# Layer 2 of a two-layer graph network: the projection of 400 turned nodes a product, with a copy and transposes behind it

## The chip, the cores and the metric

The kernel runs on one core of one Trainium2 chip. The metric is the device time of one execution in microseconds. The five engines are TensorE (PE in the profile; PEld are its weight loads), VectorE (DVE), ScalarE (ACT), GpSimd (POOL) and SyncE (SP), which only starts transfers here.

## What is computed

50,000 nodes with 128 features each and 50,000 edges, sorted by their target, go through two layers. Layer 1 is attention over the edges. Layer 2, which the change touches, is this (cut to what matters):

```python
def _L1_gnn_ref(node_features, senders, receivers, edge_features, W_kernel, W_bias, We_kernel, We_bias):
    hW = node_features @ W_kernel + W_bias
    h_self, h = jnp.split(hW, 2, axis=-1)
    send_edges = h[senders]
    send_edges = send_edges + (edge_features @ We_kernel + We_bias)
    in_degree = jax.ops.segment_sum(jnp.ones_like(receivers), receivers, num_nodes).astype(jnp.float32)
    send_edges = send_edges * jnp.clip(in_degree[receivers], 1, None)[..., None]
    return h_self + jax.ops.segment_sum(send_edges, receivers, num_nodes)

h = jnp.maximum(_layernorm(x, axis=-1), 0.0)
x = x + _L1_gnn_ref(h, src, dst, edge_attr_64, ...)
```

All in float32.

## The kernel before, in words

The nodes are cut into 500 tiles of 100 nodes, and ten tiles make a batch: 50 batches (`BATCHES`), numbered k. A tile's edges lie in one window of 128 edges. Three stages follow each other: a table of keys and values for all nodes, layer 1, and layer 2.

Since sums over edges and matrix products can change places, layer 2 first sums the raw rows that the edges bring and projects afterwards. A matrix `member` (128 edges x 100 nodes, the node's degree where edge and node belong together) does the sum. For a batch k of layer 2:

- SP loads the batch's own rows of x (`nodes1`) and the ten windows of edge features (`features`, L679, ten transfers, each with an address from a register loaded before it), two batches ahead. It stores the batch before it (`store1`, L690) when DVE's `sums` are through. It takes these in order: nodes1(k+2), registers and features(k+2), store1(k-1).
- POOL gathers the source rows of each tile (`gathers1`, L784), one indirect transfer a tile, into four slots. A pair of gathers waits until ACT has used the slot's old rows, so the gathers of k+4 go at the pace of ACT in k.
- ACT normalizes and clips a tile's own rows (L1576) and its gathered rows (L1579). It works one batch ahead of PE into single buffers `hn1` and `hs1`: the tiles 2j and 2j+1 of the next batch wait for `rows_sum(k, j)`, through the semaphore R.ha.
- PE makes in `rows_sum(k, j)` for two tiles the transposed own rows (L1869) and the summed gathered rows (L1870), in `features_sum(k, i)` for five tiles the summed edge features (L1858), and in `project1(k, g)` the result: for each tile three products into one place, with the turned rows as weights and W1 or We moving (L1884 to L1886). The groups g hold the tiles 0 to 3, 4 to 7, and 8 and 9 (`FOURS`).
- DVE makes `member` for the batch after (L1271), copies what rows_sum and features_sum left in PSUM to SBUF (`rows_out`, L1280; `features_out`, L1288), and adds x to the projected result (`sums`, L1298).

Every engine's order is written out by hand in its `step1`; nothing is planned at run time. PE's is: features_sum(k, 0), rows_sum(k, 0), project1(k-1, 2), rows_sum(k, 1), features_sum(k, 1), rows_sum(k, 2), project1(k, 0), rows_sum(k, 3), rows_sum(k, 4), project1(k, 1). DVE's is, with pairs of `member` between: features_out(k, 0), rows_out(k, 0), sums(k-1, 2), rows_out(k, 1), features_out(k, 1), rows_out(k, 2), rows_out(k, 3), sums(k, 0), rows_out(k, 4), sums(k, 1). Project1(k, g) waits for rows_out (R.ha_sb), features_out (R.ae_sb) and for the sums of two groups before (R.y).

On PE the batches 2 to 45 run in a loop of eleven turns over four batches; the others, and all batches on the other engines, are written out. In PSUM the eight banks are used so: rows_sum 0 and 1, features_sum 2 and 3, project1 4 and 5. Banks 6 and 7 are free in layer 2.

Of the kernel before, what the change touches and what calls it, by code (L numbers as in the profile page):

```python
# [16 lines left out]
NODES = 100  # L17
# [69 lines left out]


def rows_used(n):

    return 3 * (n // 5) + (1, 1, 2, 2, 3)[n % 5] if n >= 0 else 0


def features_used(n):

    return 3 * (n // 2) + (2, 3)[n % 2] if n >= 0 else 0
# [38 lines left out]
def build(nc, x, edges, ea, Wq, bq, Wk, bk, Wv, bv, Ws, bs, W1, b1, We, be, out):  # L135
# [7 lines left out]
    with ExitStack() as ctx:  # L143
# [89 lines left out]
        haT = hT_raw[:, 0:4 * 4 * NODES].rearrange("c (s t h n) -> c s t h n", s=4, t=2, h=2)  # L233
        aeT = mT_raw[0:EW + 1, 0:4 * 5 * NODES].rearrange("c (s t n) -> c s t n", s=4, t=5)
# [174 lines left out]
        class Message:  # L409


            def __init__(self):
# [10 lines left out]
                self.ae_sb = s("features_copied")  # L423
                self.out = s("out_ready")
# [369 lines left out]
        def _(dve):  # L794
# [481 lines left out]
            def rows_out(k, j):  # L1276
                n = 5 * k + j
                dve.wait_ge(R.ha, n + 1)
                wait(dve, R.out, rows_used(n - 4))
                dve.tensor_copy(haT[:, n % 4, :, :, :],  # L1280
                                banks[n % 2][:, 0:4 * NODES].rearrange("c (t h n) -> c t h n", t=2, h=2)
                                ).then_inc(R.ha_sb, 1)

            def features_out(k, i):
                n = 2 * k + i
                dve.wait_ge(R.ae, n + 1)
                wait(dve, R.out, features_used(n - 4))
                dve.tensor_copy(aeT[0:EW, n % 4, :, :],  # L1288
                                banks[2 + n % 2][0:EW, 0:5 * NODES].rearrange("c (t n) -> c t n", n=NODES)
                                ).then_inc(R.ae_sb, 1)  # L1290

            def sums(k, g):
                first, last = FOURS[g]
                dve.wait_ge(R.out, 3 * k + g + 1)
                if g == 0:
# [3 lines left out]
                                  banks[4 + (3 * k + g) % 2][0:NODES, 0:(last - first) * D]  # L1299
# [3 lines left out]
            def step1(k):  # L1303
                this, prev, nxt = real(k), real(k - 1), real(k + 1)
                if this:
                    features_out(k, 0)
                    rows_out(k, 0)
                if nxt:
                    members1(k + 1, 0, 2)
                if prev:  # L1310
                    sums(k - 1, 2)
                if this:
                    rows_out(k, 1)
                    features_out(k, 1)
                if nxt:
# [5 lines left out]
                if this:  # L1321
                    rows_out(k, 3)
                    sums(k, 0)
# [6 lines left out]
                if this:  # L1330
                    sums(k, 1)
# [301 lines left out]
        def _(pe):  # L1633
# [228 lines left out]
            def rows_sum(s, j):  # L1862
# [4 lines left out]
                for t in (2 * j, 2 * j + 1):  # L1867
                    at = (t % 2) * 2 * NODES
                    nc.tensor.transpose(banks[n % 2][:, at:at + NODES], hn1[:, t, :], ident[0:NODES, 0:NODES])  # L1869
                    ins = nc.tensor.matmul(banks[n % 2][:, at + NODES:at + 2 * NODES], hs1[:, t, :],  # L1870
# [3 lines left out]
            def project1(s, g):  # L1874
# [3 lines left out]
                pe.wait_ge(R.ae_sb, s.count(2, (1, 2, 2)[g]))  # L1878
                wait(pe, R.y, s.count(3, g - 1))
                ps = banks[4 + (3 * k + g) % 2]  # L1880
                for t in range(first, last):
                    to = ps[0:NODES, (t - first) * D:(t - first + 1) * D]
                    n = (5 * k + t // 2) % 4
                    nc.tensor.matmul(to, haT[:, n, t % 2, 0, :], w1[:, 0:D], start=True, stop=False)  # L1884
                    nc.tensor.matmul(to, haT[:, n, t % 2, 1, :], w1[:, D:2 * D], start=False, stop=False)  # L1885
                    ins = nc.tensor.matmul(to, aeT[:, (2 * k + t // 5) % 4, t % 5, :], weaug[0:EW + 1, 0:D],  # L1886
                                           start=False, stop=True)
                ins.then_inc(R.out, 1)

            def step1(s):  # L1890
# [5 lines left out]
                if prev:  # L1896
                    project1(before, 2)
                if this:
                    rows_sum(s, 1)
                    features_sum(s, 1)  # L1900
                    rows_sum(s, 2)
                    project1(s, 0)
                    rows_sum(s, 3)
                    rows_sum(s, 4)
                    project1(s, 1)
# [85 lines left out]
```

## Time and profile before

| | us |
|---|---|
| median of 3 runs | 2192.9 |
| lowest and highest | 2182.47, 2200.33 |
| the profiled execution's own time | 2195.36 |
| its span | 2193.6 |

| engine | busy us | share of the span |
|---|---|---|
| PE | 1629.7 | 74% |
| PEld | 1511.4 | 69% |
| DVE | 1322.2 | 60% |
| ACT | 1026.1 | 47% |
| POOL | 988.5 | 45% |

The span runs from the first to the last instruction. Shares are averages over three stages with different limits; layer 2 takes the last 930 us or so of the span. The granted clock of TensorE over the whole span was 0.886 of full speed. A matmul's start in the trace is recorded and its end modelled; the idle time before an instruction and what ended it stand in square brackets. "remote" or "another core or an unknown queue" as releaser means that the trace saw nothing that ended at that moment.

### The profile page before, as it was taken

How to read it: one execution, taken by the hardware profiler on the slowest of the kernel's cores; microseconds unless marked ns; L12 is line 12 of the kernel's file. 1: busy time of each engine (PE TensorE's matmuls, PEld its weight loads, DVE VectorE, ACT ScalarE, POOL GpSimd, SP SyncE). 2: the span in 40 equal slices, each digit the busy share in tenths (PEclk: the TensorE clock that was granted, in tenths of full speed). 3: DMA queues.
4: the chain of work that ended last, by engine and by line, in shares of the span. 5: the costliest groups of instructions: out<-in, count | busy, mean ns of one | idle time of the engine just before them, and what ended most of it. 6: DMA issues, size and time to landing. Idle time of an engine off the chain costs nothing.

```text
span 2193.6 us, 37235 instructions
## 1 busy us (share of the span) xinstructions
PE 1629.7 (74%) x12145; PEld 1511.4 (69%) x12146; DVE 1322.2 (60%) x3827; ACT 1026.1 (47%) x2500; POOL 988.5 (45%) x1021
## 2 busy tenths in 40 slices
PE   5879965787777787777876237777777777777787
PEld 4667754777677777767775237777777777777787
DVE  8998932787777787877778024444444444444445
ACT  5668953444444444444441224444444444444443
POOL 0100025565566556656660655545554445455530
PEclk9999986999999999999999568888888888888889
DMA  8778972454545545545441434444444444444442
GB/s 232 241 247 287 305 232 80 131 147 137 144 141 146 148 129 145 151 136 144 142 136 57 108 71 113 110 108 110 108 108 106 104 106 108 109 111 110 110 102 64
DMA packets 162400, 302.88 MB, mean 138 GB/s; under 512 B 104085, under 2 KB 107675, under 8 KB 157246
## 3 DMA queue, kind: packets, MB, share of 16 engines
q1 hardware_dynamic: 121349, 201.19, 31.9%
q0 software_dynamic: 40896, 99.90, 18.7%
q8 instruction: 64, 1.05, 0.2%
q14 instruction: 91, 0.74, 0.1%
HBM read 196.84 MB, written 104.12 MB: 137 GB/s over the span
## 4 chain that ended last, share of the span: by engine, by line
PE 38%; DVE 23%; another core or an unknown queue 20%; issue 14%; DMA 2%; ACT 2%; SPq 0%; DVEq 0%; ACTq 0%
PE ps_b L1762 6%; PE ps_b L1884 5%; PE ps_b L1858 4%; PE ps_b L1886 4%; PE ps_b L1885 4%; PE ps_b L1663 4%; DVE sb_hT L1280 3%; DVE sb_member L1271 2%; DVE sb_member L1062 2%; PE ps_b L1795 2%; PE ps_b L1750 2%; PE ps_b L1640 1%; DVE sb_alpha L1082 1%; DVE sb_xo L1134 1%
## 5 line engine op out<-in xcount | busy, mean ns | idle before, releaser
L756 POOL DMA_INDIRECT sb_kv<-kv_rows,sb_src_all x500 | 502.6, 1005 | 542.8 <-DMA kv_rows<-sb_kv 205.2
L784 POOL DMA_INDIRECT sb_kv<-x_rows,sb_src_all x500 | 473.2, 946 | 495.5 <-ACT sb_vw L1579 316.6
L1576 ACT ACTIVATE sb_hn<-sb_xn 100x128 f32<-100x128 f32 x500 | 241.4, 483 | 582.6 <-remote 307.2
L1884 PE MATMUL ps_b<-sb_w,sb_hT 128*100 128x128 f32 x1000 | 241.5, 330 | 210.7 <-DVE sb_hT L1280 198.8
L1280 DVE COPY sb_hT<-ps_b 128x400 f32<-128x400 f32 x250 | 141.8, 567 | 325.4 <-remote 295.0
L1884 PEld LDWEIGHTS ps_b<-sb_w,sb_hT 128*100 128x100 f32 x1000 | 172.6, 209 | 221.2 <-issue 211.5
L1579 ACT ACTIVATE sb_vw<-sb_kv 128x128 f32<-128x128 f32 x500 | 239.5, 479 | 0.0
L1504 ACT ACTIVATE sb_hn<-sb_xn,sb_nstat 100x128 f32<-100x128 f32 x500 | 231.2, 494 | 12.9 <-DMA sb_xn<-in_x 12.9
L1886 PE MATMUL ps_b<-sb_weaug,sb_memberT 66*100 66x128 f32 x1000 | 231.6, 319 | 7.3 <-issue 7.3
L1885 PE MATMUL ps_b<-sb_w,sb_hT 128*100 128x128 f32 x1000 | 230.9, 319 | 4.9 <-issue 4.9
L1663 PE MATMUL ps_b<-sb_w,sb_memberT 128*125 128x256 f32 x800 | 203.7, 395 | 15.1 <-DVE sb_kv L861 11.0
L1298 DVE TENSOR_TENSOR sb_xo<-ps_b,sb_xn 100x512 f32<-100x512 f32 x150 | 89.6, 597 | 172.7 <-PE ps_b L1886 151.7
L1795 PE MATMUL ps_b<-sb_vw,sb_member 128*100 128x128 f32 x1000 | 138.5, 289 | 67.3 <-DVE sb_vw L1122 67.3
L1870 PE MATMUL ps_b<-sb_member,sb_vw 128*128 128x100 f32 x1000 | 172.5, 275 | 16.9 <-issue 16.9
L1885 PEld LDWEIGHTS ps_b<-sb_w,sb_hT 128*100 128x100 f32 x1000 | 175.7, 207 | 5.1 <-issue 5.1
L1886 PEld LDWEIGHTS ps_b<-sb_weaug,sb_memberT 66*100 66x100 f32 x1000 | 174.3, 206 | 6.5 <-issue 6.5
L1795 PEld LDWEIGHTS ps_b<-sb_vw,sb_member 128*100 128x100 f32 x1000 | 122.4, 177 | 77.2 <-DVE sb_vw L1122 77.2
L1526 ACT COPY sb_memberT<-ps_b 100x512 f32<-100x512 f32 x150 | 76.2, 508 | 211.9 <-PE ps_b L1750 120.8
L1663 PEld LDWEIGHTS ps_b<-sb_w,sb_memberT 128*125 128x125 f32 x800 | 148.7, 196 | 37.0 <-issue 13.2
L1074 DVE TENSOR_TENSOR sb_prod<-ps_b,sb_kv 128x512 f32<-128x512 f32 x150 | 89.4, 597 | 128.3 <-PE ps_b L1762 119.5
L1870 PEld LDWEIGHTS ps_b<-sb_member,sb_vw 128*128 128x128 f32 x1000 | 154.0, 194 | 16.4 <-issue 16.4
L1869 PE MATMUL ps_b<-sb_ident,sb_hn 100*128 100x100 f32 x500 | 126.5, 253 | 22.2 <-issue 22.1
(169 smaller groups left out, 3198.1 us busy)
## 6 DMA issues: line engine op xcount, KB each, us to landing
kv_rows<-sb_kv SPq DMA_DIRECT2D x27, 1120.0 KB
sb_xn<-x_rows SPq DMA_DIRECT2D x50, 507.8 KB
sb_xn<-in_x SPq DMA_DIRECT2D x50, 500.0 KB
out_rows<-sb_xo SPq DMA_DIRECT2D x49, 500.0 KB
x_rows<-sb_xo SPq DMA_DIRECT2D x24, 1015.6 KB
sb_kv<-in_edge_attr SPq DMA_DIRECT2D x500, 32.0 KB
sb_kv<-in_x SPq DMA_DIRECT2D x28, 560.0 KB
kv_rows<-sb_xn SPq DMA_DIRECT2D x13, 1120.0 KB
```

The lines of the kernel that those rows point to most:

```text
L756: pool.indirect_dma_start(out=kvs[:, k % 4, t, :], out_offset=None, in_=kv_rows, in_offset=bass.IndirectOffsetOnAxis(ap=src_all[:, n:n + 1 ...
L784: pool.indirect_dma_start(out=xs1[:, k % 4, t, :], out_offset=None, in_=x1, in_offset=bass.IndirectOffsetOnAxis(ap=src_all[:, n:n + 1], ax ...
L1280: dve.tensor_copy(haT[:, n % 4, :, :, :], banks[n % 2][:, 0:4 * NODES].rearrange("c (t h n) -> c t h n", t=2, h=2)).then_inc(R.ha_sb, 1)
L1504: nc.scalar.activation(hn[:, t, :], xn[:, k % 5, t, :], ACT.Relu, scale=nstat[:, n, 0:1], bias=nstat[:, n, 1:2]).then_inc(A.relu, 1)
L1576: nc.scalar.activation(hn1[:, t, :], xn1[:, k % 4, t, 0:D], ACT.Relu, scale=xn1[:, k % 4, t, D:D + 1], bias=xn1[:, k % 4, t, D + 1:XW]).th ...
L1579: nc.scalar.activation(hs1[:, t, :], xs1[:, k % 4, t, 0:D], ACT.Relu, scale=xs1[:, k % 4, t, D:D + 1], bias=xs1[:, k % 4, t, D + 1:XW]).th ...
L1663: ins = nc.tensor.matmul(banks[2 + n % 4][0:ROWS, (t % 2) * 2 * D:(t % 2 + 1) * 2 * D], hpT[:, (3 * b + g) % 4, (t - first) * ROWS:(t - fi ...
L1795: ins = nc.tensor.matmul(ps[0:NODES, (t - first) * D:(t - first + 1) * D], member[:, k % 3, t, :], vw[:, t, :], start=False, stop=t == las ...
L1870: ins = nc.tensor.matmul(banks[n % 2][:, at + NODES:at + 2 * NODES], hs1[:, t, :], member[:, (k + 3) % 4, t, :], start=True, stop=True)
L1884: nc.tensor.matmul(to, haT[:, n, t % 2, 0, :], w1[:, 0:D], start=True, stop=False)
L1885: nc.tensor.matmul(to, haT[:, n, t % 2, 1, :], w1[:, D:2 * D], start=False, stop=False)
L1886: ins = nc.tensor.matmul(to, aeT[:, (2 * k + t // 5) % 4, t % 5, :], weaug[0:EW + 1, 0:D], start=False, stop=True)
```

## The change

Before, a product had the turned rows of one tile (100 nodes) as its weights and gave nodes by features at once. Now the weights are W1's two halves and We, and the turned nodes of a whole group move through them: 400 columns in the groups 0 and 1, 200 in group 2, three products a group instead of three a tile. This gives features by nodes. So DVE copies it to SBUF (`turned_out`, into a new view `oT`), PE turns it back tile by tile (`turn_back`, transposes into the banks 6 and 7), and `sums` reads it there. `haT` and `aeT` are laid out by group and batch, so that a group's nodes lie side by side. Two semaphores are new, R.oT and R.oT_sb; R.out now comes from turn_back. Rows_out and features_out wait for R.oT in place of R.out.

```diff
-        haT = hT_raw[:, 0:4 * 4 * NODES].rearrange("c (s t h n) -> c s t h n", s=4, t=2, h=2)
-        aeT = mT_raw[0:EW + 1, 0:4 * 5 * NODES].rearrange("c (s t n) -> c s t n", s=4, t=5)
+        haT = hT_raw[:, 0:3 * 8 * NODES].rearrange("c (g h t n) -> c g h t n", g=3, h=2, t=4)
+        aeT = mT_raw[0:EW + 1, 0:2 * B * NODES].rearrange("c (s t n) -> c s t n", s=2, t=B)
+        oT = q_raw[:, 0:3 * 4 * NODES].rearrange("c (g t n) -> c g t n", g=3, t=4)
...
             def rows_out(k, j):
                 dve.wait_ge(R.ha, n + 1)
-                wait(dve, R.out, rows_used(n - 4))
-                dve.tensor_copy(haT[:, n % 4, :, :, :],
-                                banks[n % 2][:, 0:4 * NODES].rearrange("c (t h n) -> c t h n", t=2, h=2)
+                wait(dve, R.oT, 3 * (k - 1) + j // 2 + 1)
+                at = 2 * (j % 2)
+                dve.tensor_copy(haT[:, j // 2, :, at:at + 2, :],
+                                banks[n % 2][:, 0:4 * NODES].rearrange("c (h t n) -> c h t n", h=2, t=2)
...
+            def turned_out(k, g):
+                first, last = FOURS[g]
+                dve.wait_ge(R.oT, 3 * k + g + 1)
+                wait(dve, R.out, 3 * (k - 1) + g + 1)
+                dve.tensor_copy(oT[:, g, 0:last - first, :],
+                                banks[4 + (3 * k + g) % 2][:, 0:(last - first) * NODES]
+                                .rearrange("c (t n) -> c t n", n=NODES)).then_inc(R.oT_sb, 1)
...
                 pe.wait_ge(R.ha_sb, s.count(5, last // 2))
                 pe.wait_ge(R.ae_sb, s.count(2, (1, 2, 2)[g]))
+                wait(pe, R.oT_sb, s.count(3, g - 1))
+                to = banks[4 + (3 * k + g) % 2][:, 0:(last - first) * NODES].rearrange("c (t n) -> c t n", n=NODES)
+                nc.tensor.matmul(to, w1[:, 0:D], haT[:, g, 0, 0:last - first, :], start=True, stop=False)
+                nc.tensor.matmul(to, w1[:, D:2 * D], haT[:, g, 1, 0:last - first, :], start=False, stop=False)
+                nc.tensor.matmul(to, weaug[0:EW + 1, 0:D], aeT[:, k % 2, first:last, :], start=False, stop=True
+                                 ).then_inc(R.oT, 1)
+
+            def turn_back(s, g):
+                pe.wait_ge(R.oT_sb, s.count(3, g + 1))
                 wait(pe, R.y, s.count(3, g - 1))
-                for t in range(first, last):
-                    nc.tensor.matmul(to, haT[:, n, t % 2, 0, :], w1[:, 0:D], start=True, stop=False)
-                    nc.tensor.matmul(to, haT[:, n, t % 2, 1, :], w1[:, D:2 * D], start=False, stop=False)
-                    ins = nc.tensor.matmul(to, aeT[:, (2 * k + t // 5) % 4, t % 5, :], weaug[0:EW + 1, 0:D],
-                                           start=False, stop=True)
+                for t in range(last - first):
+                    ins = nc.tensor.transpose(banks[6 + (3 * k + g) % 2][0:NODES, t * D:(t + 1) * D],
+                                              oT[:, g, t, :], ident[:])
                 ins.then_inc(R.out, 1)
```

The orders afterwards, new pieces in capitals. PE: features_sum(k, 0), rows_sum(k, 0), project1(k-1, 2), TURN_BACK(k-1, 1), rows_sum(k, 1), features_sum(k, 1), TURN_BACK(k-1, 2), rows_sum(k, 2), project1(k, 0), rows_sum(k, 3), rows_sum(k, 4), TURN_BACK(k, 0), project1(k, 1). DVE: features_out(k, 0), rows_out(k, 0), TURNED_OUT(k-1, 2), sums(k-1, 1), rows_out(k, 1), features_out(k, 1), sums(k-1, 2), rows_out(k, 2), rows_out(k, 3), TURNED_OUT(k, 0), rows_out(k, 4), sums(k, 0), TURNED_OUT(k, 1), with the pairs of `member` between as before.

## Rows read from the trace of the kernel before

**Rows 1.** The page, busy tenths in 40 slices of 54.8 us: granted clock.
```profile
PEclk9999986999999999999999568888888888888889
```
**Rows 2.** Who waited for whom, 1400 to 2100 us: total us, times, longest.
```profile
DVE sb_hT L1280 <- remote: 231.0, 38, 6.4
```
**Rows 3.** Order of time, DVE: start us, us; the first and last of these stalls.
```profile
1293.22 0.57 DVE L1280 COPY sb_hT<-ps_b 128x400 f32<-128x400 f32 x1 [13.91 <-remote]
2116.01 0.57 DVE L1280 COPY sb_hT<-ps_b 128x400 f32<-128x400 f32 x1 [5.95 <-remote]
```
**Rows 4.** Stretches: us, PE, PEld, DVE, ACT, POOL busy (count), PEclk, DMA share, GB/s.
```profile
2142.29:2154.00 11.71, 11.66 (x112) 11.50 (x111) 8.11 (x20) 8.02 (x20) 0.00 (x0) 1.00 0.40 118
```
**Rows 5.** Order of time, all engines, one batch of 50.
```profile
1703.74 0.74 PE L1884 MATMUL ps_b<-sb_w,sb_hT 128*100 128x128 f32 x2 [4.32 <-DVE sb_hT L1280]
...
1704.86 0.94 POOL L784 DMA_INDIRECT sb_kv<-x_rows,sb_src_all  x1 [3.45 <-ACT sb_vw L1579]
...
1708.33 0.38 PE L1886 MATMUL ps_b<-sb_weaug,sb_memberT 66*100 66x128 f32 x2
...
1708.75 0.69 DVE L1298 TENSOR_TENSOR sb_xo<-ps_b,sb_xn 100x512 f32<-100x512 f32 x1 [3.19 <-issue]
...
1709.81 0.38 PE L1870 MATMUL ps_b<-sb_member,sb_vw 128*128 128x100 f32 x2
...
1710.80 0.49 ACT L1576 ACTIVATE sb_hn<-sb_xn 100x128 f32<-100x128 f32 x1 [4.67 <-PE ps_b L1870]
...
1712.53 0.56 DVE L1280 COPY sb_hT<-ps_b 128x400 f32<-128x400 f32 x1
1712.63 0.35 SPq L690 DMA_DIRECT2D out_rows<-sb_xo  x1
1712.71 0.94 POOL L784 DMA_INDIRECT sb_kv<-x_rows,sb_src_all  x1 [3.17 <-ACT sb_vw L1579]
...
1716.49 0.38 PE L1870 MATMUL ps_b<-sb_member,sb_vw 128*128 128x100 f32 x2
...
1718.95 0.94 POOL L784 DMA_INDIRECT sb_kv<-x_rows,sb_src_all  x1 [0.30 <-issue]
...
1721.46 0.57 DVE L1280 COPY sb_hT<-ps_b 128x400 f32<-128x400 f32 x1 [6.30 <-remote]
1721.95 0.68 DVE L1298 TENSOR_TENSOR sb_xo<-ps_b,sb_xn 100x512 f32<-100x512 f32 x1
1722.26 0.74 PE L1884 MATMUL ps_b<-sb_w,sb_hT 128*100 128x128 f32 x2 [4.76 <-DVE sb_hT L1280]
```
**Rows 6.** The next batch: order of time (SP, POOL), chain of waits (DVE).
```profile
1731.48 0.35 SPq L690 DMA_DIRECT2D out_rows<-sb_xo  x1
1738.00 0.94 POOL L784 DMA_INDIRECT sb_kv<-x_rows,sb_src_all  x1 [0.30 <-issue]
1740.54 0.59 DVE sb_hT L1280
```
**Rows 7.** Order of time, the last four gathers of the kernel.
```profile
2117.93 0.94 POOL L784 DMA_INDIRECT sb_kv<-x_rows,sb_src_all  x1 [3.55 <-ACT sb_vw L1579]
...
2121.37 0.38 PE L1886 MATMUL ps_b<-sb_weaug,sb_memberT 66*100 66x128 f32 x2
...
2121.66 0.94 POOL L784 DMA_INDIRECT sb_kv<-x_rows,sb_src_all  x1 [0.30 <-issue]
...
2123.62 0.69 DVE L1298 TENSOR_TENSOR sb_xo<-ps_b,sb_xn 100x512 f32<-100x512 f32 x1 [5.00 <-remote]
```
**Rows 8.** Chain of waits: two instructions of a product, at half and full clock.
```profile
1705.33 0.43 PE ps_b L1884 x2
...
1729.67 0.22 PE ps_b L1884 x2
```
**Rows 9.** Order of time, table stage: 256 columns moving, and four transposes.
```profile
149.79 0.59 PE L1663 MATMUL ps_b<-sb_w,sb_memberT 128*125 128x256 f32 x2
150.22 0.59 PE L1640 MATMUL ps_b<-sb_ident,sb_q 125*128 125x125 f32 x4
```

More of the change, by code:

```diff
@@ L423, in __init__ @@
                 self.ae_sb = s("features_copied")
+                self.oT = s("turned_out_ready")
+                self.oT_sb = s("turned_out_copied")
                 self.out = s("out_ready")
@@ L1298, in sums @@
                 dve.tensor_tensor(y1[:, k % 4, first:last, :],
-                                  banks[4 + (3 * k + g) % 2][0:NODES, 0:(last - first) * D]
+                                  banks[6 + (3 * k + g) % 2][0:NODES, 0:(last - first) * D]
                                   .rearrange("n (t c) -> n t c", c=D),
@@ L1307, in step1 @@
                     rows_out(k, 0)
+                if prev:
+                    turned_out(k - 1, 2)
                 if nxt:
@@ L1310, in step1 @@
                 if prev:
-                    sums(k - 1, 2)
+                    sums(k - 1, 1)
                 if this:
@@ L1314, in step1 @@
                     features_out(k, 1)
+                if prev:
+                    sums(k - 1, 2)
                 if nxt:
@@ L1322, in step1 @@
                     rows_out(k, 3)
-                    sums(k, 0)
+                    turned_out(k, 0)
                 if nxt:
@@ L1330, in step1 @@
                 if this:
-                    sums(k, 1)
+                    sums(k, 0)
+                    turned_out(k, 1)
             def long_node_stats(S):
@@ L1867, in rows_sum @@
                 for t in (2 * j, 2 * j + 1):
-                    at = (t % 2) * 2 * NODES
+                    at = (t % 2) * NODES
                     nc.tensor.transpose(banks[n % 2][:, at:at + NODES], hn1[:, t, :], ident[0:NODES, 0:NODES])
-                    ins = nc.tensor.matmul(banks[n % 2][:, at + NODES:at + 2 * NODES], hs1[:, t, :],
+                    ins = nc.tensor.matmul(banks[n % 2][:, at + 2 * NODES:at + 3 * NODES], hs1[:, t, :],
                                            member[:, (k + 3) % 4, t, :], start=True, stop=True)
@@ L1897, in step1 @@
                     project1(before, 2)
+                    turn_back(before, 1)
                 if this:
@@ L1900, in step1 @@
                     features_sum(s, 1)
+                if prev:
+                    turn_back(before, 2)
+                if this:
                     rows_sum(s, 2)
@@ L1904, in step1 @@
                     rows_sum(s, 4)
+                    turn_back(s, 0)
                     project1(s, 1)
```

13 lines of the change are left out of this document (4 added, 9 removed).

## The prediction

> **What bounds the kernel now.** The page comes first. Its clock row falls from 9 to 5 where layer 2 begins, at about 1,290 us, and stays at 8: TensorE is halted again and again [rows 1]. The waits of 1400 to 2100 us say by what: 38 times DVE waited for something "remote" before L1280, 231 us in all [rows 2]. The stall comes once a batch. It ends at 1293.22 us first and at 2116.01 us last, 44 periods of 18.70 us [rows 3]. In the last batches, for which POOL has no gathers left, it is gone, and one takes 11.71 us with PE busy 11.66 of them [rows 4]. So PE's own work is 11.7 us, and 7 us a batch are a stall and what the half clock after it costs.
>
> What is this stall? Rows_out(k, 3) and relu1(k+1, 6) both wait for one event, the semaphore of rows_sum(k, 3). Its last matmul ended at 1716.87 us, yet DVE starts at 1721.46 and PE, which needs DVE's copy, at 1722.26 [rows 5]. The matmul was done and its signal came 4.6 us late. What happens beside it is POOL: six gathers follow one another from 1712.71 us, the last ends at 1719.89, and the signal arrives 1.57 us later. In the next batch the last gather ends at 1738.94 and DVE starts at 1740.54, 1.60 later [rows 6]. Without an output store near it, a matmul ended at 2121.75 us, POOL's last gather at 2122.60, and DVE, which waited for it, started at 2123.62 [rows 7]. I read this as: **TensorE's signals are held while a run of gathers lasts**, and come 1.0 to 1.6 us after its end. Not from its first moment: the matmul that ended at 1708.71, 3.85 us after the first gather of a run, was seen at 1708.75 [rows 5]. A run ends by itself, since gathers wait for ACT, ACT for the held signal.
>
> That gives the loop that sets the period. From PE's resumption at 1703.74: four tiles' products, features and rows_sum(0) until 1710.03 (6.29 us); ACT sees them at 1710.80 (0.77); two tiles of ACT, then the first gather (1.91); six gathers (7.18); the hold's tail (1.57); DVE's copy and PE at 1722.26 (0.80) [rows 5]. Sum 18.52, which is that batch. The other PE work of a batch lies under the six gathers.
>
> **The change, part by part.** Sizes of matmuls first. A product is two instructions; two take 0.22 us at the full clock and 0.43 at half, for 128 moving columns [rows 8]: 0.86 and 1.68 ns a column and instruction. Two with 256 columns took 0.43 us [rows 9], the same 0.84 ns, so columns set the price and the weight load is hidden. I price 400 by it: 0.34 us at full, bounded below by the 0.22 of a pair of 128 (were only starts to count) and above by 400 x 1.68 = 0.67 (half clock). A transpose is one instruction: four of 125 columns take 0.59 us with the last one's latency [rows 9], so 0.15 each at most; by its columns it is 0.11, which I take.
> Removed a batch: 30 products, 60 instructions of 128 columns, 7680 columns, 6.6 us. Added: 9 products, 18 instructions, 6000 columns, 5.16 us, and 10 transposes of 128 columns, 1.10 us. Net -0.35 us of PE at the full clock. (Ten features_sum instructions of 100 columns are 0.87; the 11.66 us of rows 4 less 6.6 and two of these leave 0.66 for each rows_sum. A project1(k, 2) will be 1.0, a turn_back of four 0.43, of two 0.22.) **On the loop** stand only project1(k, 1), before 24 x 128 = 3072 columns, now 6 x 400 = 2400, and turn_back(k, 0) ahead of it, 512: 160 columns fewer, at half clock -0.27 us a batch. The rest of the -0.35 lies under the gathers: worth nothing.
> Added on DVE: three copies a batch, two of 128x400 (0.57 us each, [rows 5], L1280) and one of 200 columns, which I take at 0.3 (between 0 and 0.57). DVE has 3.6 us idle even in an 11.71 us batch [rows 4]. Two of them cost nothing: PE does not wait for them, and if DVE were later they would stretch the store only. The third does: after the stall DVE copies rows (3), then turned_out(k, 0), and PE stands at turn_back(k, 0) until that second copy is done. The instruction behind such a copy starts 0.49 us after it (1721.46 and 1721.95, [rows 5]). **Cost +0.48 us a batch, on the loop.** Behind this wait stand project1(k, 1) and the next features_sum; ACT waits for rows_sum(k+1, 0) behind those.
> Moved: sums(k, 0) and (k, 1) go later; sums(k-1, 2), which releases SP's store and node load, now follows features_out(k, 1). From rows_sum(0) to the store there are 1.0 + 0.43 + 0.66 + 0.87 us of PE, then 0.7 and 0.35 of DVE: 4.2 us with gaps, where the trace has 2.6 (1710.03 to 1712.63). The store, the node load, ten register loads and ten edge loads on SP all start 1.6 us later. Their data are for two batches on: hidden, unless the rival below holds. The banks 6 and 7 and the slot counts add no wait, since each refers to a result of a batch or two groups before.
> Without stalls (five batches) -0.35 of work meets +0.35 of waiting for turned_out(k, 0): nothing. The tail gains one copy and two transposes, +1 us.
> **Sum:** 44 x (0.48 - 0.27) = +9, +1 at the end: +10 us on the profiled execution's 2195.4 us, which is 2.5 us above the median of 2192.9. **Forecast 2206 us.** The bounds of the two loop terms, -0.5 to 0 and +0.2 to +0.6, give 2184 to 2222.
>
> Does the added DVE work slow the gathers? Beside the copy that ran at 1712.53 to 1713.09 the gather took 0.94 us, the same as at 1718.95, when DVE had nothing to do [rows 5]; I add nothing. The Trainium skill, SBUF — State Buffer, section "Who interferes with whom", says that DVE copies in a two-port mode lock GpSimd out of a shared port while it writes descriptors. By that rule, which this row does not bear out, the change would come out slower.
>
> **The rivals.**
> *Slower: the hold ends with SP's burst, not with the gathers.* For it: DVE starts 8.83 us after the store's issue at 1712.63 and 9.06 after that at 1731.48 [rows 5, 6], nearly as fixed as my 1.57 and 1.60. Against: the 0.23 between those two is just by how much the gathers moved, and rows 7 show a hold with no store within 15 us. If it is so, the store's 1.6 us (2.4 in the other kind of batch, where it now follows rows_sum(0) by 1.8) is added to the loop: 2.0 + 0.2 = +2.2 us a batch, +97 us, **2293 us**. It decides as soon as the tail is longer than 1.6 us after the last gather.
> *Slower: gathers are locked out by DVE.* Two copies a batch of 0.57 in the run of gathers would add 1.1 us to it: +50 us, 2255. Against it stands the 0.94 above. It is the SBUF page's rule as a mechanism here.
> *Slower: the clock stays at half.* Today it is back at full some 6 us after PE resumes (0.43 at 1705.33, 0.22 at 1729.67, [rows 8]). PE's work from rows_sum(0) to its stop, 7.2 us, has 11.4 us of cover; at half it needs 14.4 and sticks out by 3.0: +132 us, 2338. Nothing in the rows speaks for it, so I give it little.
> *Faster: the signal of rows_sum(k, 3) slips through.* Project1(k, 0) shrinks from 2.64 to 2.06 us and transposes come ahead of it. Rows_sum(k, 3) ended 4.2 us after the first gather; now, counted from rows_sum(0): 1.0 + 0.43 + 0.66 + 0.87 + 0.22 + 0.66 + 2.06 + 0.66 + 0.17 = 6.7, less 2.0 to 2.7 for the first gather, 4.0 to 4.7. The trace has one signal passed at 3.85 and one held at 3.82 [rows 5, 7]. Where it passes, the 4.8 us stop and part of the half clock go: 14.5 us for such a batch. Every second one: 44 x -2.1 = -92, **2103 us**; all: 2010.
> *It does not take effect:* the 400-column products could cost more than their columns; even at the bound of 0.67 they stay under the gathers except six a batch: +2 us x 44, inside the slower case.
>
> **How the numbers follow.** Forecast 0.45, store burst 0.18, lockout 0.05, clock 0.04, slip 0.25 (half of it at every second batch), small mixes 0.03. A change within 1% (22 us) can't be told from none: same 2171 to 2215. The forecast puts 0.40 there and 0.05 above; with the mixes: same 0.42, slower 0.33, faster 0.25. The likeliest case's own range is 2184 to 2222; the range for 8 in 10 goes on to the burst above and to the slip in every second batch below: 2100 to 2295. It leaves out the full slip and the clock.
>
> **What would show it.** Right: DVE's wait before rows_out(k, 3) still some 6 us, released 1.5 us after the last gather's end, six gathers in the run, a second DVE copy before PE resumes 1.3 us after the release, PE's busy time 0.3 to 0.5 us lower a batch, a period near 18.9. Wrong: a release that keeps 8.8 us from the store (burst), gathers above 0.94 us (lockout), clock 0.5 for longer than 7 us (clock), or runs of eight gathers and periods under 17 us (slip). It would fall altogether if the hold went by something that these rows don't show, the position in PE's program for one.

## The result

| us | before | after |
|---|---|---|
| median | 2192.3 (4 runs, 2182.47 to 2200.33) | 2117.41 (4 runs, 2111.76 to 2121.28) |
| profiled execution, its span | 2195.36, 2193.6 | 2121.28, 2119.4 |
| PE busy | 1629.7 | 1596.5 |
| DVE busy | 1322.2 | 1390.2 |

The ratio is 0.9647, 95% interval 0.9617 to 0.9678: 75 us faster. The forecast was 2206. The range of 2100 to 2295 holds the time, but the sign is wrong. No case of the prediction describes the batch that most of layer 2 now repeats; nearest in time is the slip of every second batch, 2103.

The page after, its clock row (slices of 53.0 us) and the gathers' group (busy us, mean ns of one | idle before), to be read against [rows 1]:
```profile
PEclk9989996999999999999999757999888888777789
...
L777 POOL DMA_INDIRECT sb_kv<-x_rows,sb_src_all x500 | 473.3, 947 | 420.1 <-ACT sb_vw L1586 228.8
```
The waits after, 1400 to 2060 us, against [rows 2]:
```profile
DVE sb_hT L1274 <- remote: 120.8, 34, 3.7
```
The stall is still there, in nearly every batch, but it lasts 3.7 us and not 6.3. One steady batch in order of time, against [rows 5]:
```profile
1700.04 1.09 PE L1899 MATMUL ps_b<-sb_ident,sb_q 128*100 128x128 f32 x4 [3.22 <-issue]
...
1700.85 0.95 POOL L777 DMA_INDIRECT sb_kv<-x_rows,sb_src_all  x1 [1.88 <-ACT sb_vw L1586]
...
1702.26 1.54 PE L1889 MATMUL ps_b<-sb_hT,sb_w 128*128 128x400 f32 x2
...
1703.59 1.54 PE L1890 MATMUL ps_b<-sb_memberT,sb_weaug 66*128 66x400 f32 x2
...
1706.40 0.38 PE L1877 MATMUL ps_b<-sb_member,sb_vw 128*128 128x100 f32 x2
...
1706.90 0.50 ACT L1583 ACTIVATE sb_hn<-sb_xn 100x128 f32<-100x128 f32 x1 [4.77 <-PE ps_b L1877]
...
1708.83 0.95 POOL L777 DMA_INDIRECT sb_kv<-x_rows,sb_src_all  x1 [3.27 <-ACT sb_vw L1586]
...
1710.82 0.35 SPq L683 DMA_DIRECT2D out_rows<-sb_xo  x1
...
1712.87 0.38 PE L1877 MATMUL ps_b<-sb_member,sb_vw 128*128 128x100 f32 x2
...
1715.08 0.95 POOL L777 DMA_INDIRECT sb_kv<-x_rows,sb_src_all  x1 [0.30 <-issue]
1716.03 0.57 DVE L1274 COPY sb_hT<-ps_b 128x400 f32<-128x400 f32 x1 [3.73 <-remote]
1716.03 0.49 ACT L1583 ACTIVATE sb_hn<-sb_xn 100x128 f32<-100x128 f32 x1 [3.44 <-remote]
1716.31 2.52 SPq L672 DMA_DIRECT2D sb_kv<-in_edge_attr  x4
...
1716.52 0.56 DVE L1290 COPY sb_q<-ps_b 128x400 f32<-128x400 f32 x1
...
1717.14 1.09 PE L1899 MATMUL ps_b<-sb_ident,sb_q 128*100 128x128 f32 x4 [3.27 <-issue]
...
1717.95 0.95 POOL L777 DMA_INDIRECT sb_kv<-x_rows,sb_src_all  x1 [1.92 <-ACT sb_vw L1586]
```
The run still has six gathers. But DVE and ACT are released at 1716.03, which is the moment at which the last gather ends (1715.08 + 0.95), and not 1.5 us behind it. From the first gather of the four to that of the next four, in pieces: 6.05 until ACT has rows_sum(0), 1.93 to the first of six gathers, 7.20 to the release, 1.92 to the next gather: 17.10. The same pieces before [rows 5] are 5.94, 1.91, 8.75 and 1.92 (PE's resumption at 1722.26 and the 1.12 from it to a gather): 18.52. **The difference is in one piece, 8.75 to 7.20**; the others add 0.13. The store rows of 44 batches span 823.4 us before and 747.5 after, 75.8 less, which is the whole gain of 74 us on the profiled execution. The last 30 of them, from 1540 us on, are such steady batches of 17.07 us and gain 51.6. The first 14 gain 24.2 in another way: they vary between 14.7 and 18.8 us, 16.8 in the mean, and their gathers come in runs of two to ten.

### The profile page after: what moved, and what is told of

It is laid out like the page before. It is cut to its first block, busy times and chain, and to the rows that moved or that the text cites. A ratio compares the mean times of both kernels' runs of the same rounds, so it can differ in the third digit from the quotient of the medians.

```text
span 2119.4 us, 34578 instructions
## 1 busy us (share of the span) xinstructions
PE 1596.5 (75%) x10545; PEld 1337.9 (63%) x10546; DVE 1390.2 (66%) x3977; ACT 1036.2 (49%) x2500; POOL 990.1 (47%) x1021
## 3 DMA queue, kind: packets, MB, share of 16 engines
q0 software_dynamic: 40896, 99.90, 18.7%
q8 instruction: 62, 1.02, 0.2%
## 4 chain that ended last, share of the span: by engine, by line
PE 47%; DVE 19%; issue 17%; another core or an unknown queue 10%; DMA 2%; ACT 2%; SPq 1%; DVEq 0%; ACTq 0%
PE ps_b L1769 6%; PE ps_b L1877 5%; PE ps_b L1888 5%; PE ps_b L1889 5%; PE ps_b L1890 5%; PE ps_b L1865 4%; PE ps_b L1899 4%; PE ps_b L1670 3%; DVE sb_member L1055 2%; PE ps_b L1802 2%; PE ps_b L1876 2%; PE ps_b L1757 2%; DVE sb_st L833 1%; DVE sb_kv L854 1%
## 5 line engine op out<-in xcount | busy, mean ns | idle before, releaser
L1511 ACT ACTIVATE sb_hn<-sb_xn,sb_nstat 100x128 f32<-100x128 f32 x500 | 231.7, 495 | 13.7 <-DMA sb_xn<-in_x 13.7
L1899 PE MATMUL ps_b<-sb_ident,sb_q 128*100 128x128 f32 x500 | 99.8, 324 | 156.6 <-issue 111.7
L1899 PEld LDWEIGHTS ps_b<-sb_ident,sb_q 128*100 128x100 f32 x500 | 64.1, 149 | 170.1 <-issue 124.8
L1290 DVE COPY sb_q<-ps_b 128x400 f32<-128x400 f32 x150 | 75.1, 501 | 130.7 <-PE ps_b L1890 66.3
L1264 DVE TENSOR_SCALAR sb_member<-sb_iota,sb_drel_all,sb_wdeg_all 128x100 f32<-128x100 f32 x500 | 144.2, 335 | 0.0
L1865 PEld LDWEIGHTS ps_b<-sb_member,sb_kv 128*65 128x65 f32 x1000 | 109.5, 156 | 53.4 <-issue 36.3
L1888 PE MATMUL ps_b<-sb_hT,sb_w 128*128 128x400 f32 (+1 forms) x300 | 137.4, 545 | 5.3 <-issue 4.3
L1525 ACT COPY sb_q<-ps_b 100x512 f32<-100x512 f32 x150 | 76.3, 509 | 132.6 <-remote 88.8
```

What stands on the lines that cost most here:

```text
L1511: nc.scalar.activation(hn[:, t, :], xn[:, k % 5, t, :], ACT.Relu, scale=nstat[:, n, 0:1], bias=nstat[:, n, 1:2]).then_inc(A.relu, 1)
L1865: ins = nc.tensor.matmul(banks[2 + n % 2][0:EW, (t - 5 * i) * NODES:(t - 5 * i + 1) * NODES], eaw[:, k % 4, t, :], member[:, (k + 3) % 4, ...
L1888: nc.tensor.matmul(to, w1[:, 0:D], haT[:, g, 0, 0:last - first, :], start=True, stop=False)
L1899: ins = nc.tensor.transpose(banks[6 + (3 * k + g) % 2][0:NODES, t * D:(t + 1) * D], oT[:, g, t, :], ident[:])
```

## The experiments

Each result is compared with the kernel before on the same chip. That turned out to matter more than anything else: on some chips TensorE's signals were held beside gathers, on others not. The runs that held ran on three chips, those that did not on five; for the first result the chip is not known. Only one chip was met twice (e15 and e17, not held both times), so whether this is fixed for a chip or a state that it can leave is not shown. Layer 1, which gathers too, differs as well: the second store of layer 2 comes at 1321 us in the profile before and at 1072 in e17.

| runs | the kernel before there | signals |
|---|---|---|
| first result | 2192 | held |
| e1 to e4; e8 to e11; e12, e13 | 1679.6; 1680.8; 1681.0 | not held |
| e5 to e7 | 2153.6 | held |
| e14 | 2196.1 | held |
| e16 | 2152.2 | held |
| e15; e17; e18 | 1682.3; 1679.1; 1682.6 | not held |

**e1 to e4: SP's transfers and DVE's order, first attempt.** The first suspicion was SP: the store's place against the gathers had moved by 2 us, and the edge loads had moved behind the last gather.
```diff
 e1   wait(sp, R.ae, 2 * (k - 3))
+     if k >= 3: sp.wait_ge(R.ha, 5 * (k - 3) + 4)     # ahead of the ten edge loads
 e2  +  if k >= 1: sp.wait_ge(R.ha, 5 * (k - 1) + 4)   # ahead of the register loads
 e3  +  held = window_registers(k + 3)                 # behind features(k + 2), which uses the last `held`
 e4   rows_out(k, 3); turned_out(k, 0)  ->  turned_out(k, 0); rows_out(k, 3)
```


> The kernel before, with one wait more on SP: the ten edge loads of a batch wait for rows_sum(k, 3)'s signal, which is what rows_out(k, 3) is held up for; the ten register loads stay where they are. Theory A (edge loads): in the kernel before the edge loads begin at 1717.95 us, with the last two gathers of the run still to come (1717.70, 1718.95), and they add the 1.5 us between the last gather's end and the release; in the changed kernel they begin at 1716.31, after the run's end at 1716.03, and that is what the change won. Then here the tail falls from 1.5 to about 0, the period from 18.7 to about 17.2, and the time to about 2126 us (2192 less 44 x 1.5). Theory B (store and row load: their 1 MB starts 0.1 us after the first gather of the run before, 2.0 us after it in the changed kernel): nothing changes here, 2192 us, tail 1.5.

> The kernel before, with SP's wait ahead of the ten register loads too, so that beside the run of six gathers SP issues only the store and the row load. The register loads take 4.4 to 5.6 us for ten beside the gathers and 0.5 where there are none. Theory A (edge loads): as with the edge loads alone late, about 2126 us, since the register loads have no part. Theory C (register loads have a part in the hold): better than that by a measurable amount, the hold starts later or not at all, 2000 to 2100 us. Theory B (store and row load): 2192 us.

> The changed kernel, with each batch's ten register loads made one batch ahead, so that the ten edge loads are issued right behind the row load, in the middle of the run of gathers, instead of after it. Theory A (edge loads): the tail comes back, 1.5 us or more a batch, period 18.6 or more, about 2185 us. Theory B (store and row load): the tail stays 0, 2117 us. Theory C (register loads prolong the hold): they now come behind the edge loads, nearer to the release, so no gain, 2117 us or up to 1 us a batch more (2160).

> The changed kernel, with DVE's copy of the turned result, turned_out(k, 0), ahead of rows_out(k, 3), which is the one that is held up. It takes the copy's 0.5 us, which the prediction put on the loop, off it: either the copy's own signal comes before the hold, and PE needs one copy less after it, or it comes with it, and PE starts turn_back(k, 0) 0.5 us sooner while DVE does the other copy. Expected if the copy stands on the loop: period 17.07 less 0.5 is 16.6, about 2095 us. If DVE's order is hidden: 2117 us. If the extra wait at the head of DVE's queue costs something because members1 and the other copies stand behind it: over 2117 us.

Measured: 1680.24, 1679.55, 1677.65 and 1678.49 us, ratios to before 1.0001, 0.9999, 0.9988 and 0.9991, each within 0.15% of 1. No theory was tested, since there was no hold. What the runs do show is the changed kernel's worth where nothing is held: e3 and e4 are the changed kernel with a small edit, and their 0.1% is not clear of nothing (0.9973 to 1.0003 and 0.9976 to 1.0006).

**e5 to e7: the changed kernel again, and both kernels without gathers.** E6 and e7 load neighbouring rows of the same table instead; what they leave out is that the rows are those that the edges name.
```diff
-  pool.indirect_dma_start(out=xs1[:, k % 4, t, :], ..., in_=x1, in_offset=...)
+  at = min(n * NODES, N - 128)
+  pool.dma_start(xs1[:, k % 4, t, :], x1[at:at + 128, :])
```


> The changed kernel itself, unaltered, because in e1 to e4 the kernel before took 1680 us and not 2192: there, TensorE's signals come 0.01 us after the matmul's end beside runs of gathers, and no batch has a stall. If a machine without the hold runs this too: the change is then worth only what it does to the engine that bounds a batch. Theory P (POOL bounds: ten gathers of 0.945 us and 0.30 of issue are 12.5 us): no change, ratio 0.997 to 1.003. Theory Q (PE bounds, with 11.87 us a batch before and some 0.35 less after): 45 x 0.35 = 16 us less, ratio 0.990. If the hold is back: ratio 0.965, as first measured.

> The kernel before, with the 500 gathers of layer 2 replaced by plain loads of 128 neighbouring rows of the same table, issued by POOL at the same points under the same waits; what is left out is that the rows are those the edges name. Where signals are held: theory 'the gathers hold the signals' says the stall is gone and every batch takes what the last ones took, 11.7 us, so 2192 - 44 x 7.0 = 1885 us; theory 'any transfer that lands beside PE's work holds them' says 2192. Where they are not held, theory P (POOL bounds a batch) says the batch falls from 12.5 us to PE's 11.87, some 1650 us; theory Q (PE bounds) says no change, 1680.

> The changed kernel with the same plain loads in place of layer 2's gathers. With no gathers PE is what bounds both kernels, so against e6 this measures what the change does to PE's work and waits alone. By the prediction's columns -0.35 us a batch, if the wait for turned_out(k, 0) is hidden: 17 us less than e6. If that wait of 0.5 us shows in each batch: 0 to 8 us more than e6.

Measured: e5 2084.39 (ratio 0.9682, 0.9655 to 0.9709), e6 1816.92 (0.8438, 0.8407 to 0.8468), e7 1812.93 (0.8423, 0.8392 to 0.8454). On a chip that holds signals the gain is there again, and without the gathers of layer 2 both kernels lose their stalls at once: **the gathers are what holds the signals**, not transfers as such. Layer 2 then repeats in 11.87 us (e6) and 11.76 (e7). Stretch 1400 to 1700 us of e6, columns as in [rows 4], and PE's wait in it, columns as in [rows 2]:
```profile
1400.00:1700.00 300.00, 294.66 (x2785) 290.61 (x2783) 206.76 (x507) 203.01 (x505) 134.16 (x252) 1.00 0.73 171
```
```profile
PE ps_b L1883 <- DVE sb_hT L1279: 5.3, 25, 0.2
```
The same two of e7:
```profile
1400.00:1700.00 300.00, 286.31 (x1978) 232.78 (x1978) 235.50 (x588) 208.45 (x512) 136.38 (x257) 1.00 0.72 173
```
```profile
PE ps_b L1898 <- DVE sb_q L1289: 13.7, 26, 0.5
```
PE's busy time a batch falls by 0.44 us (294.66/300 of 11.87 is 11.66, 286.31/300 of 11.76 is 11.22), and its wait grows from 0.21 (5.3/25) to 0.53 (13.7/26). With PE as the bound, fewer columns and one more copy to wait for leave 0.11 us a batch.

**e8 to e13: the same questions, and again no hold.**
```diff
 e8, e12    sp.wait_ge(R.y, 3 * (k + 1))
+           sp.wait_ge(R.ha_sb, 5 * (k + 1) + 3)       # store1 waits for rows_out(k, 2)
 e9         as e1
 e10        PE: turn_back(k-1, 2), DVE: sums(k-1, 2), both ahead of the work on rows_sum(k, 1)
 e11, e13   as e4
```


> The kernel before, products and order of DVE and PE unaltered, with one wait more on SP: the store, and behind it the row load, the register loads and the edge loads, wait for DVE's rows_out(k, 2), which puts this burst some 2.0 us after the first gather of the run of six instead of 0.1 us, just where the changed kernel has it. Where TensorE's signals are held beside gathers (before at 2150 to 2190 us): theory A (place of SP's burst against the gathers): the release comes with the last gather's end and no longer 1.5 us behind it, 44 x 1.5 = 66 us less, 3% less, and the wide products have no part in the gain. Theory D (the gain is PE's, fewer columns and signals at other moments): no change. Where signals are not held (before at 1680): within 0.3%, since nothing waits for SP.

> The kernel of e1, for which no signals were held, once more, for the case that they are here. The ten edge loads alone wait for rows_sum(k, 3)'s signal. Theory A1 (of SP's burst it is the edge loads, issued into the last two gathers, that add the 1.5 us): as much gained as in e8, 3%. Theory A2 (it is the 1 MB of store and row load): no change, ratio 0.997 to 1.003.

> The changed kernel with turn_back(k-1, 2) and sums(k-1, 2) moved ahead of rows_sum(k, 1), so that SP's burst begins 1.0 us earlier, 1.0 us after the first gather of the run. Same instructions, same counts. Theory A: a part or all of the 1.5 us a batch comes back, up to 66 us or 3% over the changed kernel's ratio of 0.965 to 0.968: 0.98 to 1.00 against before. Theory D: 0.965 to 0.97 as it was.

> The kernel of e4 once more, for the case that signals are held here: turned_out(k, 0) ahead of rows_out(k, 3). If the second copy after the release stands on the loop, as the prediction had it with 0.48 us, the period falls by 0.5 us: 22 us, ratio to before 0.955 to 0.958 where the changed kernel has 0.965 to 0.968. If DVE's order is hidden: 0.965 to 0.968.

> The kernel of e8 once more, for which no signals were held. SP's burst of a batch waits for rows_out(k, 2), 2.0 us after the first gather of the run instead of 0.1 us. Where signals are held (before at 2150 to 2190 us): theory A (place of SP's burst): 1.5 us a batch less, ratio 0.965 to 0.975, without any of the wide products. Theory D (the gain is PE's): 0.997 to 1.003. Where they are not held: 1.000.

> The kernel of e4 and e11 once more, for the case that signals are held. If the copy turned_out(k, 0) stands on the loop with 0.5 us a batch: ratio 0.955 to 0.958 to the kernel before, where the changed kernel has 0.965 to 0.968. If not: 0.965 to 0.968. Where signals are not held: 0.999.

Measured: 1680.05, 1681.0, 1680.02, 1677.42, 1682.51 and 1680.45; ratios 0.9996, 0.9997, 1.0002, 0.9988, 1.0006, 0.9988, all intervals within 0.3% of 1. In order of time, e12, a chip without the hold:
```profile
1410.08 0.95 POOL L785 DMA_INDIRECT sb_kv<-x_rows,sb_src_all  x1 [0.30 <-issue]
...
1412.58 0.95 POOL L785 DMA_INDIRECT sb_kv<-x_rows,sb_src_all  x1 [0.31 <-issue]
...
1413.69 0.38 PE L1871 MATMUL ps_b<-sb_member,sb_vw 128*128 128x100 f32 x2
1413.83 0.94 POOL L785 DMA_INDIRECT sb_kv<-x_rows,sb_src_all  x1 [0.30 <-issue]
1414.11 0.57 DVE L1281 COPY sb_hT<-ps_b 128x400 f32<-128x400 f32 x1 [0.18 <-PE ps_b L1871]
```
The matmul ends at 1414.07 in the midst of a long run of gathers, and DVE starts 0.04 us later. The gathers cost what they did, 0.95 and 0.30 between. They now follow each other without a pause: ten are 12.5 us, and 43 batches took 12.60 us each in this run, 12.42 to 12.59 in e1, e3, e4, e10, e11 and e13. POOL is the bound there, in both kernels, and PE's saving has nothing to shorten.

**e14: SP's part, four ways in one trace.** The variants of e1, e2 and e8 stand in stretches of the same kernel.
```diff
+  if 13 <= k + 1 < 23: sp.wait_ge(R.ha_sb, 5 * (k + 1) + 3)    # whole burst late
+  if 23 <= k - 3 < 33: sp.wait_ge(R.ha, 5 * (k - 3) + 4)       # edge loads late
+  if 33 <= k - 1 < 43: sp.wait_ge(R.ha, 5 * (k - 1) + 4)       # register and edge loads late
```


> The kernel before, with SP's waits different in four stretches of layer 2, so that one trace compares them. Steps 3 to 12: as before. 13 to 22: the whole burst (store, row load, register loads, edge loads) waits for rows_out(k, 2), 2.0 us after the run's first gather. 23 to 32: only the edge loads wait, for rows_sum(k, 3)'s signal. 33 to 42: register loads and edge loads wait for that signal. Where signals are held, the period of the first stretch is 18.7 us. Theory A1 (edge loads issued into the last gathers add the 1.5 us): 18.7, 17.1, 17.1, 17.1. Theory A2 (the place of the store and the row load does): 18.7, 17.1, 18.7, 18.7. Theory C (register loads beside the gathers have a part in the hold): the fourth under the third by 1 us or more. Theory D (SP's burst has no part, the gain is PE's): 18.7 four times. Where signals are not held: 12.3 to 12.7 four times.

Measured: 2194.42, ratio 0.9993 (0.9981 to 1.0005). In order of time, the stores at the bounds of the stretches, and a run of gathers in the second and in the fourth:
```profile
1338.29 0.35 SPq L694 DMA_DIRECT2D out_rows<-sb_xo  x1
...
1527.83 0.35 SPq L694 DMA_DIRECT2D out_rows<-sb_xo  x1
...
1600.75 0.94 POOL L790 DMA_INDIRECT sb_kv<-x_rows,sb_src_all  x1 [3.21 <-ACT sb_vw L1585]
...
1603.24 0.36 SPq L694 DMA_DIRECT2D out_rows<-sb_xo  x1
...
1609.44 0.58 DVE L1286 COPY sb_hT<-ps_b 128x400 f32<-128x400 f32 x1 [5.79 <-remote]
...
1713.84 0.35 SPq L694 DMA_DIRECT2D out_rows<-sb_xo  x1
...
1901.58 0.35 SPq L694 DMA_DIRECT2D out_rows<-sb_xo  x1
...
1976.26 0.94 POOL L790 DMA_INDIRECT sb_kv<-x_rows,sb_src_all  x1 [3.23 <-ACT sb_vw L1585]
...
1984.93 0.57 DVE L1286 COPY sb_hT<-ps_b 128x400 f32<-128x400 f32 x1 [5.80 <-remote]
...
1986.23 0.90 SPq L681 DMA_DIRECT2D sb_kv<-in_edge_attr  x2
...
2089.31 0.35 SPq L694 DMA_DIRECT2D out_rows<-sb_xo  x1
```
Ten batches each: 18.95, 18.60, 18.77, 18.77 us. The store itself moves by some 2 us into the second stretch and out of it, so the first two are 18.7 and 18.8 without that. With the store 2.5 us behind the first gather, as in the changed kernel, the release still comes 8.69 after that gather; with register and edge loads behind the release, 8.67. **SP has no part in it**: theories A1, A2 and C fall.

**e15 and e16: PE's and DVE's order in the changed kernel.**
```diff
+  14 <= k < 26:  DVE turned_out(k, 0) ahead of rows_out(k, 3)
+  26 <= k < 46:  PE rows_sum(s, 3) ahead of project1(s, 0)
```


> The changed kernel with three stretches of layer 2 that differ. Steps 2 to 13: as it is. 14 to 25: DVE's copy turned_out(k, 0) ahead of rows_out(k, 3). 26 to 45: PE does rows_sum(k, 3) ahead of project1(k, 0), so that its signal is given some 2.8 us after the run's first gather and not 4.4. e14 has shown that SP's burst has no part in the tail, and its trace and those of before and after show releases at 1.44 us times a whole number after the run's first gather: 8.65 (six) in the kernel before, 7.16 (five) in the changed one. Theory L (a ladder: each gather blocks TensorE's signals for 1.44 us, they pass only at a rung, and which rung depends on when PE gives them): third stretch released at a lower rung, 2.9 to 5.8 us after the first gather, its period shorter than 17 by 1.4 us or more, or irregular with runs of eight or ten gathers, 15 to 16.5 in the mean. Theory W (the rung is the last or last but one of the run whatever PE does): third stretch as the first, 17.1. For the copy: 0.5 us less in the second stretch if it stands on the loop, 0 if not. Where signals are not held: 12.4 in all three.

> The kernel of e15 once more, for which no signals were held (1682 us, as the kernel before). Where they are held: theory L (a ladder of 1.44 us rungs, the rung set by when PE gives the signal): stretch of steps 26 to 45, with rows_sum(k, 3) ahead of project1(k, 0), released at a lower rung or irregular, mean period 15 to 16.5 against 17.1 in steps 2 to 13; theory W: 17.1 as well. Copy first, steps 14 to 25: 16.6 if the copy stands on the loop, 17.1 if not.

Measured: e15 1682.18 (1.0002, no hold); e16 2090.04, ratio 0.9708 (0.9668 to 0.9747). The stores at the bounds, e16:
```profile
1307.14 0.35 SPq L683 DMA_DIRECT2D out_rows<-sb_xo  x1
...
1504.32 0.36 SPq L683 DMA_DIRECT2D out_rows<-sb_xo  x1
...
1703.11 0.36 SPq L683 DMA_DIRECT2D out_rows<-sb_xo  x1
...
2019.67 0.35 SPq L683 DMA_DIRECT2D out_rows<-sb_xo  x1
```
12, 12 and 19 batches: 16.43, 16.57 and 16.66 us. The unaltered changed kernel of e5, on another such chip, has 16.58, 16.38 and 16.71 in the same three. Neither the copy's place nor the earlier signal (by the product's length, some 2 us) moves the mean by more than 0.2. Theory L, as far as it said that an earlier signal wins time, falls for these means; the copy's 0.5 us does not show either. Both edits were met only where the changed kernel never settles: its batches take 14.6 to 18.7 us to the end in e5, and on neither chip do the steady batches of 17.07 come. What the edits do to those is not tested.

**e17 and e18: PE's order in the kernel before.**
```diff
+  14 <= k < 26:  rows_sum(s, 3), rows_sum(s, 4), project1(s, 0)
+  26 <= k < 46:  rows_sum(s, 3), project1(s, 0), rows_sum(s, 4)
```


> The kernel before, with three stretches of layer 2 that differ in PE's order alone; products as before. Steps 2 to 13: project1(k, 0), rows_sum(k, 3), rows_sum(k, 4), as it is; the first of these signals is given 3.5 or 4.0 us after the run's first gather, the release comes at 8.65, six times 1.44. 14 to 25: rows_sum(k, 3), rows_sum(k, 4), project1(k, 0), so that the two signals that ACT and DVE wait for are given 2.6 us earlier. 26 to 45: rows_sum(k, 3), project1(k, 0), rows_sum(k, 4). e16 has shown that in the changed kernel neither DVE's copy order nor this order of PE moves the mean period, 16.4 to 16.6 in all three. Theory L (the moment at which PE gives its signals sets the rung, and that is how the change won): 18.7 in the first stretch and 16.4 to 17.2 in one of the others or both, with the products as they were. Theory N (it takes the narrow products away to win): 18.5 to 18.8 in all three. Where signals are not held: 12.4 to 12.6 in all three.

> The kernel of e17 once more, for which no signals were held. Three stretches of the kernel before that differ in PE's order alone. Where signals are held: theory L (the moment of PE's signals sets the rung): 18.0 to 18.8 in steps 2 to 13, 16.4 to 17.2 in 14 to 25 or 26 to 45 or both. Theory N (it takes the narrow products away to win): 18.0 to 18.8 in all three.

Measured: 1681.64 (1.001) and 1681.76 (0.9996), both without the hold: inconclusive.

## What a release waits for

The traces of the chips that hold say more than the prediction had read. Run of ten gathers, e5, order of time:
```profile
1381.32 0.95 POOL L777 DMA_INDIRECT sb_kv<-x_rows,sb_src_all  x1 [2.98 <-ACT sb_vw L1586]
...
1387.01 0.57 DVE L1274 COPY sb_hT<-ps_b 128x400 f32<-128x400 f32 x1 [0.59 <-remote]
...
1392.58 0.95 POOL L777 DMA_INDIRECT sb_kv<-x_rows,sb_src_all  x1 [0.31 <-issue]
1395.54 0.57 DVE L1290 COPY sb_q<-ps_b 128x400 f32<-128x400 f32 x1 [2.86 <-remote]
```
From the first gather to the release that follows the run: 5.69 us for four gathers [rows 7], 8.75 for six [rows 5], 14.22 for ten. That is 1.42 to 1.46 us a gather, where POOL issues one every 1.25. So the tail behind the last gather is not a constant of 1.0 to 1.6 us but grows with the run: 1.02 for four, 1.5 for six, 2.0 for ten (1395.54 less 1393.53).

The prediction's own trace had the strongest row for this, and the prediction showed it without using it: the stall that ends at 1293.22 us [rows 3] follows a run of 56 gathers. Before, in order of time, that run's first and last gather and PE in its midst:
```profile
1214.28 0.94 POOL L784 DMA_INDIRECT sb_kv<-x_rows,sb_src_all  x1 [60.39 <-SPq L700]
...
1249.51 0.37 PE L1885 MATMUL ps_b<-sb_w,sb_hT 128*100 128x128 f32 x1 [2.43 <-issue]
1252.31 0.37 PE L1885 MATMUL ps_b<-sb_w,sb_hT 128*100 128x128 f32 x1 [2.43 <-issue]
...
1282.94 0.94 POOL L784 DMA_INDIRECT sb_kv<-x_rows,sb_src_all  x1 [0.30 <-issue]
```
The release comes 78.94 us after the first gather, 1.41 each, and 9.3 behind the end of the last; PE's last matmul ahead of it ends at 1291.16. The rows of PE show that "signals are held" is too narrow, too: these are instructions of one product, between which the program waits for nothing, and they start 2.80 us apart, twice 1.40. In a short run PE goes on at full speed and only its signals are late; in this long one it is itself slowed.

Within a run signals get through as well, and again at multiples of this step. After, a run of ten in order of time:
```profile
1487.26 0.94 POOL L777 DMA_INDIRECT sb_kv<-x_rows,sb_src_all  x1 [3.06 <-ACT sb_vw L1586]
...
1494.49 0.57 DVE L1274 COPY sb_hT<-ps_b 128x400 f32<-128x400 f32 x1 [2.13 <-remote]
...
1501.76 0.57 DVE L1290 COPY sb_q<-ps_b 128x400 f32<-128x400 f32 x1 [3.65 <-remote]
```
That is 7.23 and 14.50, five and ten times 1.45. Other releases of this trace come 2.91, 4.39, 5.73, 8.65, 10.08 and 11.48 us after a run's first gather (two, three, four, six, seven and eight), and the 7.20 of each steady batch is the fifth. The last of its six gathers ends there too, but in the run of ten four more begin behind 7.23. Not every release fits: a few here, and over a third in e5 and e16, most of them where one run follows closely on another.

**In the 30 steady batches the change won by this: its signals pass at the fifth step, those of the kernel before at the sixth.** The kernel before did so once as well: at 1321.36 us a run of six begins whose release comes at 7.20. In the other 14 batches, and in e5 and e16 to the end, a signal often passes early enough for the run to go on to eight or ten gathers, and the batch is then shorter than 17 us. How the kernel before spends its batches on those two chips, no trace shows.

What decides at which point they pass is open. The moment of the signal alone does not. Rows_sum(k, 3) ends 4.16 us after the first gather before [rows 5] and waits for 8.75; 4.42 after it in the changed kernel (1713.25) and passes at 7.20. The kernel before has a second kind of batch, here in order of time:
```profile
1694.15 0.94 POOL L784 DMA_INDIRECT sb_kv<-x_rows,sb_src_all  x1 [3.65 <-ACT sb_vw L1579]
...
1698.41 0.38 PE L1870 MATMUL ps_b<-sb_member,sb_vw 128*128 128x100 f32 x2
...
1702.94 0.57 DVE L1280 COPY sb_hT<-ps_b 128x400 f32<-128x400 f32 x1 [5.87 <-remote]
```
There it ends at 1698.79, 4.64 after the first gather, and waits for 8.79. So the changed kernel's 4.42 lies between two that wait longer. Whether the narrow products themselves had to go, or only the rhythm that they made, is not shown: e17 and e18 were to tell it. Nor do the runs tell what the step of 1.4 us is.

## Why the prediction was wrong

- **What bounds the kernel**: right for the chips that hold. The stall, its cause in the runs of gathers and its place in the loop are confirmed by e6 and e7, which lose it with the gathers. It is no property of the kernel alone: on five chips the same program takes 1679 to 1683 us, and e12's trace has no such stall.
- **"The hold's tail (1.57)", carried over unchanged: the step that failed.** It was read from batches that are all alike, and taken for a constant behind the last gather. It measured 0.0 in the 30 steady batches after, which is -1.55 us each, 46.5 of the 51.6 us that they gained. The rest is mostly that the kernel before alternates between batches of 18.52 us and 19.07 (gathers at 1704.86, 1723.38 and 1742.45), where after all are alike. In the other 14 batches it isn't the tail but the length of the runs that differs.
- **Columns on the loop, -0.27**: the price of a column was right (two instructions of 400 at half clock take 1703.59 - 1702.26 = 1.33 us, 0.67 each, as bounded). But PE's stretch from resumption to the end of rows_sum(0) grew from 6.45 (1710.19; the prediction counted to the next start, 1710.03) to 6.74, +0.29 where the columns gave -0.27. The clock made the difference: before, PE was back at the full clock from 1708.11 on, 4.4 us after it resumed, with two instructions of a product 0.22 us apart again; after, all six instructions of 400, to 1704.92, ran at half. The granted clock of this stretch was 0.66 before and 0.61 after.
- **Second copy on the loop, +0.48**: PE does resume 1.11 us after the release instead of 0.80. Both additions, +0.29 and +0.31, cost almost nothing: ACT saw rows_sum(0) 0.61 us late before, held by the run of four gathers, and 0.12 late after. From the first of four gathers to ACT it is 5.94 and 6.05. The prediction listed this lateness as a fixed term, though it was slack. e16, where the copy's place does not change the mean, agrees; where nothing is held, PE's wait of 0.53 in e7 is 0.32 more than the 0.21 of e6, near the 0.35 forecast for such batches.
- **PE's work, -0.35 a batch**: -0.44 by busy time between e6 and e7; in batches without stalls "nothing" was forecast and -0.11 came.
- **SP's burst 1.6 us later, hidden**: right, by e14. The rival that tied the hold to the burst falls with it: the release comes 5.21 after the store, not 8.8. The lockout did not come either: with three more copies a batch a gather took 0.947 us in the mean, before 0.946. The Trainium skill, SBUF — State Buffer, section "Who interferes with whom", says that DVE copies in a two-port mode lock GpSimd out. The prediction applied this to copies that read PSUM; no run here shows in which mode they ran, so the trace neither bears the rule out nor speaks against it.
- **The slip through in every second batch**: its time was close, by luck for the most part. The steady batches, 51.6 of the 75.8 us, are not of its kind, for their runs are still six long. The first 14 are: three of their runs have ten gathers and four have eight, and seven of the 14 take under 16.2 us.

## What to carry to other kernels

A constant read from batches that are all alike is one measurement, however often it repeats: look for rows in which the run has another length (here four, six and 56 were all in the trace: 1.02, 1.5 and 9.3 behind the last gather) before it goes into a sum. A term that ends in a wait of its own may be slack, and work added ahead of it free. And a stall for which no instruction is to blame should be measured on more than one chip before a kernel is tuned around it: this change is worth 3.5% and 3.2% where signals are held, and near copies of it 0 to 0.1% where they are not, which is not clear of nothing.

## What the runs showed of the hardware

Chips, or states of chips, differ: the same program takes 2152 to 2196 us on three chips and 1679 to 1683 on five, with the same gathers (0.95 us, one every 1.25). Where signals are held, they come at a step of 1.41 to 1.46 us a gather, counted from the first of a run, and in a run of 56 gathers PE's own instructions start 2.80 us apart. In e12, without the hold, two instructions of such a product take 0.22 us beside gathers. What differs in such a chip is not known.

One expectation (e2) blamed the gathers for SP's slow register loads, which stand between its row load and its first edge load. That is not borne out. In order of time, after, when POOL had no gathers left:
```profile
2064.33 0.32 SPq L677 DMA_DIRECT2D sb_xn<-x_rows  x1
2070.25 5.04 SPq L672 DMA_DIRECT2D sb_kv<-in_edge_attr  x10
```
5.9 us lie between the two starts, where it is 5.1 beside the gathers (1711.22 and 1716.31).
